# Counting the found edges in one instruction per part, with GpSimd's subtraction and constants set later

## The reference, cut to what matters

```python
def _L0_gnn_ref(x, rows, cols, W0, b0, W1, b1):        # twice, with W0,b0 and W1,b1
    neigh = segment_sum(vals[:, None] * x[cols], rows, num_segments=N)
    return relu(concatenate([x, neigh], axis=1) @ W.T + b)
def _L1_gnn_ref(feat, W_self, W_neigh, src, dst):
    h_sparse = _maxk(feat @ W_neigh, 32)               # the 32 largest of a row, else 0
    neigh = segment_sum(h_sparse[src], dst) / maximum(deg, 1.0)[:, None]
    return feat @ W_self + neigh
x = _layernorm(x + _L0_gnn_ref(x, src, dst, ...))
x = _layernorm(x + _L1_gnn_ref(x, W_self, W_neigh, src, dst))
```

## Time and profile before

| | |
|---|---|
| median of 3 runs | 659.98 us (658.75 to 664.8) |
| the profiled execution | 660.82 us |
| its span in the trace | 659.0 us, mean granted TensorE clock 0.989 |
| slots found, branch taken | at about 33 us |
| last block built | at about 172 us |
| layers and the last sum | 172 to 659 us |

### The profile page before, as it was taken

How to read it: one execution, slowest core, us unless ns; L and a number is a source line. 1 busy time by engine, 2 the same in 40 slices (tenths; PEclk the granted TensorE clock), 3 DMA queues, 4 the chain that set the end, 5 groups by cost and what they waited for, 6 DMA issues and landing times.

```text
span 659.0 us, 10805 instructions
## 1 busy us (share of the span) xinstructions
PE 632.4 (96%) x3758; PEld 322.7 (49%) x3759; DVE 494.8 (75%) x1273; ACT 315.4 (48%) x606; POOL 111.4 (17%) x188
## 2 busy tenths in 40 slices
PE   8879999999999999999998999999999999999996
PEld 3456666776544444444443444444444444444442
DVE  7888999999759998888845588878878837533333
ACT  3678999999397777676622222222222200000000
POOL 3104221221200111001002223232232200000000
PEclk9979999999999999999999999999999999999999
DMA  8534655555522222222224999999999533300000
GB/s 212 109 97 141 225 178 184 186 172 172 160 42 64 59 69 67 53 61 58 51 52 133 189 182 201 180 185 196 174 202 177 154 99 116 111 26 26 24 24 24
DMA packets 66742, 79.62 MB, mean 121 GB/s; under 512 B 30320, under 2 KB 59407, under 8 KB 66681
## 3 DMA queue, kind: packets, MB, share of 16 engines
q1 hardware_dynamic: 66681, 78.86, 55.5%
HBM read 38.91 MB, written 33.38 MB: 110 GB/s over the span
## 4 chain that ended last, share of the span: by engine, by line
PE 63%; DVE 22%; DMA 6%; ACT 4%; POOL 3%; issue 2%; SPq 0%; ACTq 0%; DVEq 0%; POOLq 0%
PE pair L1593 21%; PE bank L1689 11%; PE pair L1689 10%; PE bank L1520 5%; DVE hots L665 4%; PE bank L1486 4%; DMA tr_sb<-part 4%; PE pair L1406 4%; DVE m L985 3%; PE bank L1494 3%; PE pair L1494 3%; DVE work L990 3%; ACT a L1273 2%; POOL part L573 2%; DVE ct L822 1%
## 5 line engine op out<-in xcount | busy, mean ns | idle before, releaser
L1593 PE MATMUL pair<-a,ct 125*128 125x512 f16 x625 | 139.5, 380 | 0.0
L1593 PE MATMUL pair<-xs,ct 125*128 125x512 f16 x625 | 139.1, 379 | 0.0
L665 DVE TENSOR_TENSOR hots<-iota,jobs 125x1792 f16<-125x1792 f16 (+1 forms) x100 | 103.7, 1073 | 0.7 <-ACT jobs L1096 0.7
L1593 PEld LDWEIGHTS pair<-a,ct 125*128 125x128 f16 x625 | 62.3, 100 | 74.6 <-issue 1.4
L1593 PEld LDWEIGHTS pair<-xs,ct 125*128 125x128 f16 x625 | 61.9, 99 | 72.5
L1114 ACT ACTIVATE slab<-pair 125x875 f16<-125x875 f32 (+1 forms) x100 | 83.3, 860 | 3.3 <-PE pair L1406 1.7
L1273 ACT ACTIVATE a<-ct 125x1000 f16<-125x1000 f16 (+1 forms) x75 | 80.4, 1072 | 1.6
L555 POOL TENSOR_TENSOR own_in<-own_in,bias_sb 125x256 f32<-125x256 f32 x50 | 37.6, 752 | 238.5 <-DMA own_in<-own_dram 238.4
L1689 PE MATMUL bank<-xs,ct 125*128 125x512 f16 (+1 forms) x325 | 71.5, 379 | 0.0
L1689 PE MATMUL pair<-xs,ct 125*128 125x512 f16 x300 | 66.2, 379 | 0.0
L1340 ACT ACTIVATE sd<-mv,epsb 125x1 f32<-125x1 f32 x25 | 7.4, 294 | 113.9 <-DVE mv L1047 113.9
(11 more groups left out here) (203 smaller groups left out, 753.7 us busy)
## 6 DMA issues: line engine op xcount, KB each, us to landing
c_dram<-slab SPq DMA_DIRECT2D x25, 683.6 KB
ct<-c_dram SPq DMA_DIRECT2D x25, 683.6 KB
own_in<-own_dram SPq DMA_DIRECT2D x50, 125.0 KB
own_dram<-own SPq DMA_DIRECT2D x25, 125.0 KB
own_dram<-own_st SPq DMA_DIRECT2D x25, 125.0 KB
x_in<-in_x_dram SPq DMA_DIRECT2D x25, 125.0 KB
z_dram<-z_st SPq DMA_DIRECT2D x25, 125.0 KB
a<-z_dram SPq DMA_DIRECT2D x5, 625.0 KB
```

What stands on the lines that cost most here:

```text
L665: v.tensor_tensor(hots[k][:, :, :, :].rearrange("p w g (a d) -> p (w g) a d", d=2), iota, job, ALU.is_equal).then_inc(win_hot, 1)
L1593: ins = mm(agg[k % 3][0:lhs.shape[1], :], lhs, parts[l][:, t, :], start=t == 0, stop=t == NT - 1, skip_group_check=True)
```

## The change

- `count(k)`: L654 and L655 become one instruction that takes the smaller of key and 1 and writes the row's sum as a second output.
- The `keep_clock` after each group of part 1's picks is gone (8 matmuls).
- POOL stops after `iota128`, until part 0 is unpacked (`cols_ready` 2). Then come the small constants and the identity's addition. The five constants of the general way come after DVE's eighth set of one-hots (`win_hot` 8) and count in a semaphore of their own, `general_ready`. Before their first write to `ct`, in iteration 1, DVE and ACT wait for it.
- `quick_hots` waits for 11 constants, L1420 on PE for 18.
- `split_a0(t)`, for `t` from 4 to 23: the subtraction waits until DVE has made all four sets of `t+1`.
- ACT does one copy of a single element before its first real instruction, so that its table is loaded then.

```diff
@@ gpsimd
             nc.gpsimd.iota(iota128[:, :], [[1, 128]], base=0, channel_multiplier=0,
                            allow_small_or_imprecise_dtypes=True).then_inc(const_ready, 1)
+            pool.wait_ge(cols_ready, 2)
             nc.gpsimd.memset(ones16[:, :], 1.0).then_inc(const_ready, 1)
...
-            nc.gpsimd.iota(iota16[:, :], [[1, KEY]], base=0, channel_multiplier=0,
-                           allow_small_or_imprecise_dtypes=True).then_inc(const_ready, 1)
...
-            pool.wait_ge(const_ready, 9)
             pool.wait_ge(ws_loaded, 16)
...
+            pool.wait_ge(win_hot, 2 * FILLS)
+            nc.gpsimd.iota(wcol[:, :], [[0, 1]], base=0, channel_multiplier=1,
+                           allow_small_or_imprecise_dtypes=True).then_inc(general_ready, 1)
...
                 pool.wait_ge(a0_hi, t + 1)
+                if 3 < t < NT - 1:
+                    pool.wait_ge(win_hot, FILLS * (t + 2))
                 nc.gpsimd.tensor_tensor(xs[:, t, F:2 * F], a0, xs[:, t, 0:F], ALU.subtract).then_inc(a0_split, 1)
...
-        NCONST = 23
+        NCONST = 18
@@ vector, count(k)
-                step(v.tensor_scalar(row_hit[:, lo:hi], row_key[:, lo:hi], 1.0, None, ALU.min))
-                v.tensor_reduce(hits[:, k:k + 1], row_hit[:, lo:hi], X, ALU.add).then_inc(count_ready, 1)
+                v.tensor_scalar(row_hit[:, lo:hi], row_key[:, lo:hi], 1.0, 0.0, ALU.min, ALU.add, accum_out=hits[:, k:k + 1]
+                                ).then_inc(count_ready, 1)
@@ vector, ahead of the first quick_hots
-            dve.wait_ge(const_ready, NCONST)
+            dve.wait_ge(const_ready, 11)
@@ vector, iteration t of the quick way
                         bound_rows()
+                        dve.wait_ge(general_ready, 5)
@@ scalar, at the start
+            act.wait_ge(warm_ready, 1)
+            a.activation(own[0:1, 0, 0:1], warm[0:1, 0:1], ACT.Copy)
@@ scalar, iteration t of the quick way
                         own_t(0)
+                        act.wait_ge(general_ready, 5)
@@ tensor, picks
                             last = mm(out, m[:, at:at + 128], pick[:, g, lo:hi],
                                       start=False, stop=g == EQ - 1 and n == 2, skip_group_check=True)
-                        if k:
-                            keep_clock(bank[7], 1)
```

More of the change, by code:

```diff
@@ L258, in gnn @@
         out3 = [bank[i] for i in (7, 2, 0, 1, 5, 6, 3, 4)]
-        const_ready = sem("const_ready")
+        const_ready, general_ready = sem("const_ready"), sem("general_ready")
         src_loaded, dst_loaded, dst_more = sem("src_loaded"), sem("dst_loaded"), sem("dst_more")
@@ L511, in _ @@
             nc.gpsimd.memset(onesq[:, :], 1.0).then_inc(const_ready, 1)
-            nc.gpsimd.iota(iota16[:, :], [[1, KEY]], base=0, channel_multiplier=0,
-                           allow_small_or_imprecise_dtypes=True).then_inc(const_ready, 1)
-            nc.gpsimd.iota(woff[:, :], [[KEY, NW]], base=0, channel_multiplier=0,
-                           allow_small_or_imprecise_dtypes=True).then_inc(const_ready, 1)
-            nc.gpsimd.iota(inc_f[:, :], [[1, EQ], [EQ, EG]], base=1, channel_multiplier=0,
-                           allow_small_or_imprecise_dtypes=True).then_inc(const_ready, 1)
-            nc.gpsimd.iota(rev_f[:, :], [[-1, EQ], [-EQ, EG]], base=CH, channel_multiplier=0,
-                           allow_small_or_imprecise_dtypes=True).then_inc(const_ready, 1)
-            nc.gpsimd.iota(wcol[:, :], [[0, 1]], base=0, channel_multiplier=1,
-                           allow_small_or_imprecise_dtypes=True).then_inc(const_ready, 1)
-            pool.wait_ge(const_ready, 9)
             pool.wait_ge(ws_loaded, 16)
@@ L526, in _ @@
                 nc.gpsimd.tensor_tensor(w_eye, w_eye, identf[:, :], ALU.add).then_inc(eye_added, 1)
+            pool.wait_ge(win_hot, 2 * FILLS)
+            nc.gpsimd.iota(wcol[:, :], [[0, 1]], base=0, channel_multiplier=1,
+                           allow_small_or_imprecise_dtypes=True).then_inc(general_ready, 1)
+            nc.gpsimd.iota(iota16[:, :], [[1, KEY]], base=0, channel_multiplier=0,
+                           allow_small_or_imprecise_dtypes=True).then_inc(general_ready, 1)
+            nc.gpsimd.iota(woff[:, :], [[KEY, NW]], base=0, channel_multiplier=0,
+                           allow_small_or_imprecise_dtypes=True).then_inc(general_ready, 1)
+            nc.gpsimd.iota(inc_f[:, :], [[1, EQ], [EQ, EG]], base=1, channel_multiplier=0,
+                           allow_small_or_imprecise_dtypes=True).then_inc(general_ready, 1)
+            nc.gpsimd.iota(rev_f[:, :], [[-1, EQ], [-EQ, EG]], base=CH, channel_multiplier=0,
+                           allow_small_or_imprecise_dtypes=True).then_inc(general_ready, 1)
             steps = [3]
@@ L726, in general_table @@
                 dve.wait_ge(win_hot, 2 * FILLS)
+                dve.wait_ge(general_ready, 5)
+                dve.sem_inc(win_hot, FILLS * NT)
                 dve.wait_ge(win_done, FILLS)
```

## The result

The changed kernel takes **652.07 us** (median of 4 runs, 651.75 to 652.62) against 660.53 for the kernel before on the same chip (658.75 to 664.8): a ratio of 0.987 with a 95% interval of 0.983 to 0.991. The forecast was 652.0. The profiled execution took 652.12 us with a span of 650.3, so its own difference to the span before, 659.0, is 8.7 us.

The account below looks back on a forecast made before the run. DVE was taken to time the building of blocks up to 166 us, PE and ACT close behind. Terms of -4.0 (start), -3.7 and -0.3 (loop) sum to -8.0, from the 660.0 median to 652; range 649.5 to 657.0.

Parts of the forecast that it names:

- Constants later, first effect, -2.1: Start: DVE's first rounding of `ends` no longer waits out POOL's constants; everything up to the first one-hots comes 2.1 us earlier.
- The identity's addition, 0: Start: POOL's addition slides from beside DVE's sets 0 and 1 to sets 2 and 3; same 0.5 us paid, no term.
- No ones between picks, -1.5: Part 1's picks: without 8 matmuls on ones, DVE's unpacking starts at 22.8 us instead of 26.41, 1.5 us of it new.
- The count, -0.4: Part 1's count on DVE: one instruction of 0.65 us replaces two costing 1.05, saving 0.4 us (bounds 0.6 and 0.4).
- The branch 4.0 earlier: End of the start: part 1's one-hots begin at about 27.0 us and the branch, hanging on the count, comes 4.0 us earlier.
- The iotas, 0: Behind the branch: POOL's five iotas end 0.6 us before ACT needs them and cost DVE's set 0 nothing; bound 1.3 us.
- The subtraction, -3.7: Loop: POOL's subtraction moved beside DVE's copy shortens iterations from 5.19 to 4.97 us, 3.7 us over 17.
- The gated iterations ahead, -0.3: The three gated iterations ahead of the 17, which carry weight splitting and leave ACT little room: 0.3 us gained.
- The loop did not stay at 5.10: Rival: PE, or the ring through PE and ACT, holds the loop at 5.10 us per iteration: 654.5 us, chance 0.20.
- The start gives half: Rival: slow clock through the picks, `ends` slow for another reason, or iotas delaying DVE: 654.2 us, chance 0.12.
- The slower rival: Loop rival: the late subtraction falls mid-set each time, +0.25 us over 20 gated iterations: 661.0 us, chance 0.04.
- more: Rival: PE's clock is up earlier around the branch and the loop runs at 4.88 us: 649.5 us, chance 0.06.

Follow-up runs that it names:

- l_const: The changed kernel with all of POOL's constants, the five iotas too, set at the start again as one train: 655.41 us, ratio 0.993.
- after_again: The changed kernel, unaltered, run once more in a later job: 652.48 us (650.51 to 655.33), ratio 0.987.
- l_table: The changed kernel without the small ACT instruction that loads the table early: 652.65 us, ratio 0.990.
- a_sub: The kernel before with only the wait ahead of POOL's subtractions in the loop added: 655.97 us, ratio 0.994.
- half_sub: The changed kernel with the gated subtraction cut into two halves of 128 columns, each meant to lie beside a DVE copy: 653.08 us, ratio 0.991.
- mid_sub: The changed kernel with POOL's subtraction released two one-hot sets earlier, in the middle of the three: 657.99 us, ratio 0.998.
- no_sub: The changed kernel with POOL writing zeros instead of the gated subtractions in 20 iterations: 654.68 us, ratio 0.991.
- l_sub: The changed kernel without the wait ahead of POOL's subtractions in the loop: 657.96 us, ratio 0.998.

## Why the prediction came true, point by point

- *What bounds the kernel.* Right: all that was gained was gained before the first matmul over blocks, 7.99 us for a sum of 8.0.
- *Constants later, first effect, -2.1.* The mechanism is shown, at 1.94 to 2.04 us (l_const). "Is something else late next?" was answered with no, and that step failed in the first profile: PE waited 1.78 us for `w_nat`, and sets 0 and 1 came at 17.54 instead of the 17.0 forecast. In after_again and l_table the load was in time and they came at 16.7. The trace of before had no wait on this load to read, but its slack there, some 1.8 us, was never worked out: it is less than the 2.1 us by which PE was to come earlier.
- *The identity's addition, 0.* Its half microsecond was to be paid under sets 2 and 3. In the first profile its load came at 20.81 and it lay beside the end of set 3 and two reductions, and sets 2 and 3 took their 1.82 us: nothing was paid. With 0.24 us saved on part 0's count (0.24 for 0.48), which the forecast had left out, this cancelled the loss to `w_nat`. In after_again it was paid in part: sets 2 and 3 take 2.08 us for 1.82.
- *No ones between picks, -1.5.* Unpacking at 22.63 for 22.8. The saving is real only beside a DVE that waits: 1.98 us with the clock down in the picks, 0.31 with it up. The forecast took before's profile, which had the clock down there, for the rule.
- *The count, -0.4.* 0.44, the new one at 0.60 for 0.65. Its bound from the sum's row was the right one to lean on. The Trainium skill, SBUF — State Buffer, section "Who interferes with whom", leaves the form that writes out its accumulator out of the fast two-port modes of `tensor_scalar`. The rows agree with that: over 125x500 in f32 the plain form takes 0.42 us, the form with the accumulator 0.68, as long as the sum.
- *The branch 4.0 earlier.* 4.24 by part 1's one-hots.
- *The iotas, 0.* Right: set 0 of `t` = 2 takes 1.09 us beside them, and ACT's first copy starts 0.44 us after their end (0.6 forecast). The rule of the Trainium skill (SBUF — State Buffer, section "Who interferes with whom") that a two-input DVE instruction does not contend with a GpSimd instruction that only writes, agrees with this; the 1.3 us taken from the row on `ends` did not carry over. That section of the Trainium skill also says that an instruction of DVE in a two-port mode does contend with GpSimd, and counts `tensor_scalar` among those that can enter one; both `ends` (2.32) and the `before` rows of l_const (3.41 for 1.91) beside memsets and iotas agree.
- *The subtraction, -3.7.* 3.07 us over the 17 iterations of the first profile, 3.3 in a_sub's, 2.3 to 3.8 over the nine profiles with the gate as written. The common iteration is 4.96, as forecast, but 4 of 17 were longer, where POOL's copy fell beside the one-hots or ACT waited for the stores of slabs. The tail in set 0 is 0.17, not 0.1.
- *The gated iterations ahead, -0.3.* 0.83, by the lead at the two copies. This term was too small: three gated iterations at 0.23 would be 0.7. Together with the 17 it is 3.9 for 4.0.
- *What would show it.* "Iterations with some idle on DVE" was wrong: DVE is busy for 83.98 of 84 us. It stands at 4.96 and the floor of the others at 4.93, so it still holds the loop, but by 0.03 us. The sum had DVE at 4.9 and ACT at 4.97, with ACT as the bound. It is the other way round: the tail in set 0 puts DVE at 4.96, and ACT can do 4.93. That the common iteration came within 0.01 us of the 4.97 is luck, since the engine named as its bound was the wrong one.
- *The rivals.* The loop did not stay at 5.10. "The start gives half" by the clock is real in one profiled execution, half_sub's. The slower rival's mechanism exists where the gate opens early (mid_sub, 5.245 per iteration), but the gate as written avoids it. A loop at 4.88, as "more" had it, is below the floor of 4.93.

The total is nearer than its terms: 0.6 us lost to `w_nat` and some 0.5 saved on the addition, 0.6 too much for the loop and 0.5 too little ahead of it. That these cancel, down to 652.07 for 652.0, is luck; executions of the same kernel lie 4.8 us apart. So is the profiled execution's 652.12 for the 652.8 that the sum gave it: 0.8 of the difference to before lies in the second layer.

## What to carry to other kernels

Before moving GpSimd's work, ask for each piece which DVE instructions lie beside it, and put pieces with two inputs beside DVE's copies out of PSUM, pieces that only write beside two-input DVE instructions: the same 0.67 us subtraction cost DVE 0.47 us inside the one-hots, 0.39 just ahead of them and 0.17 beside a copy. Before counting a saving at a wait in full, list what else that engine waits for and how early each is, loads above all. And read the floor of a loop by taking the disputed work out of it once (no_sub): it tells how much there is still to gain, here 0.03 us per iteration.

## What the runs showed of the hardware that was not expected

- A train of small GpSimd instructions that only write, 2.3 us of it, takes the same 2 us from DVE whichever `tensor_scalar` it meets: one of 4 elements per partition grows from 0.27 to 2.32 us, or a group of four from 1.91 to 3.41 with 0.45 on the one ahead.
- Where a two-input subtraction of POOL and one-hots of DVE collide, the rows fit engines that take turns by the instruction. A subtraction that asks within a set waits for its end (1.25 to 1.29 us instead of 0.67, in mid_sub and l_sub) and then costs DVE 0.47; one that is ahead of the set keeps its 0.67 us and costs DVE 0.39.
- PE's granted clock fell to 0.50 in every profile, during or just after PE's idle wait of 3.0 to 3.2 us behind the branch, and stayed down for about 7 us in nine of them, 10 in one and 13.6 in four, both 7 and 13.6 with the changed kernel itself; the difference is worth 1.8 us. Within the picks it fell in four of fourteen profiles, in one of them for all of part 0 and most of part 1 with PE busy throughout. What decides the length was not found.
